# A graph-convolution and mixture-of-experts kernel: a 512-column clear on GpSimd after each gather of result rows

## The chip, the cores and the metric

The kernel runs on one core of one Trainium2 chip. The time is the device time of one launch in microseconds (us), and the number of a kernel is the median of its runs. Five engines run their own instruction streams and meet through semaphores: TensorE (PE in the profile), VectorE (DVE), ScalarE (ACT), GpSimd (POOL) and SyncE (SP), which here only starts transfers.

## The reference

```python
# x: 8192 x 128, adj: 8192 x 8192, all float32
x = x + gnn(layernorm(x), adj)            # message passing
x = x + moe(layernorm(x))                 # 16 experts, best 2 of them for each row

# gnn:  msg = z @ W + B
#       weights = where(adj < 1, exp(-(1/adj - 1)**2 / 0.5), 0);  return weights @ msg
# moe:  logits = z @ gate_w + gate_b;  top 2 experts, softmax over the two logits
#       h = relu(z @ w1[e] + b1[e]);  out = h @ w2[e] + b2[e]     (128 -> 256 -> 128)
#       y = z + sum of the two experts' outputs by their shares
#       return layernorm(y) * gamma + beta
```

## The kernel before, in words

The 8192 rows are 16 groups of 512 rows. **The main stage** runs over the groups and, for each, over 16 chunks of 512 columns of the adjacency matrix. SP loads a chunk, VectorE and ScalarE turn its values into weights (lines 654, 660, 516, 521), TensorE transposes them (L1137), ScalarE finishes them (L527), and TensorE multiplies them with the messages (L1118). When a group is done, its rows are normalised, the gate picks two experts for each row, and GpSimd scatters the group's rows to a DRAM array `rows_in`, sorted by expert, with eight indirect transfers of 128 rows each (L476).

**The expert stage** begins when the last group is nearly through, at about 1430 us. The sorted rows are cut into 153 units, each of one expert. The groups form three batches of 7, 5 and 4 groups, with 71, 35 and 47 units; units of the second batch have 256 rows, the others 128. For each unit SP loads the rows (L374), TensorE transposes them (L1153), ScalarE copies them out (L592), TensorE makes the first layer (L1164), ScalarE applies the ReLU (L601), TensorE makes the second layer (L1192), and VectorE adds the bias (`add_bias`, L989). SP stores the results of two units at a time to the DRAM array `rows_out` (L387). VectorE also copies each unit's weights out of the table of experts (`fetch`, L980).

**Gather and combine.** A group's results lie scattered in `rows_out`. Once all the units of a batch are stored, GpSimd fetches each of its groups with eight indirect transfers (K = 2 experts for each row, times TB = 4 tiles of 128 rows). Each transfer moves 128 rows of 512 bytes (L494), into one of four buffers `back`. From the fifth group on, GpSimd waits before a group until VectorE has used the buffer (`back_free`). One tiny multiplication, `carry()` (L457), precedes the eight. VectorE then combines the group in about a dozen steps (`combine_slot`, L1004 to L1028; its layer norm uses L666, L673 and L698 to L702, with two steps on ScalarE, L533/L535 and L613), and SP stores it.

**The order** is written out by hand. Each engine runs a loop over i = 0 to 231. In step i VectorE does `add_bias(i - 1)`, `fetch(i + 7)` and the step `i - starts[g]` of every group g whose combine is under way. `starts` is a list of constants: 79, 85, 91, 97, 103, 109, 120 for the first batch, 131, 142, 153, 164, 175 for the second, 186, 197, 208, 219 for the third. Seven groups are therefore combined from step 153 on, after the last unit. VectorE executes in this order, so a combine that waits for its gather (`back_in`) holds back the units behind it. In the profile `back`, `rin` and the other buffers of this stage appear under the name `chunk`, since they are cut from the chunks' storage.

Of the kernel before, what the change touches and what calls it, by code (L numbers as in the profile page):

```python
# [13 lines left out]
P = 128  # L14
# [5 lines left out]
def gnn_moe_kernel(nc, x, adj, gnn_w, gnn_b, gate_w, gate_b, w1, b1, w2, b2, gamma, beta, out):  # L20
    N, D = x.shape
    E, _, F = w1.shape
    FT = F // P
    K = 2
# [35 lines left out]
    KB = K * TB  # L60
# [12 lines left out]
    with ctx:  # L73
        def sb(name, shape, dt=F32):
            return ctx.enter_context(nc.sbuf_tensor(name, shape, dt))

        def sem(name):
            return ctx.enter_context(nc.semaphore(name))
# [15 lines left out]
        eps = sb("eps", [P, 1])  # L94
        zeros = sb("zeros", [P, UW // P * D])
        pool_carrier = sb("pool_carrier", [1, 3])
        iota_e = sb("iota_e", [P, E])
        upto_e = sb("upto_e", [P, E, E])
        region0 = sb("region0", [P, len(BATCHES), E])
# [119 lines left out]
        rows_ready = sem("rows_ready")  # L219
        carried = sem("carried")  # L220
        scattered = sem("scattered")
        spare_zero = sem("spare_zero")
        ends_ready = sem("ends_ready")
        padded = sem("padded")
# [66 lines left out]
        def _(sp):  # L291
# [36 lines left out]
            def pad(b, e):  # L328
                if e == 0:
                    sp.wait_ge(ends_ready, b + 1)  # L330
                    sp.wait_ge(zeros_ok, 2)
                    _, values = nc.values_load_multi_w_load_instructions(
                        ends[0:1, b, :], engines=[mybir.EngineType.SP], min_val=0, max_val=BASE[-1] - UW,
                        skip_runtime_bounds_check_because="a region's start plus the rows counted in it")
                    region_ends.update(zip(range(E), values))
                sp.dma_start(rows_in[bass.ds(region_ends[e], UR[b]), :].rearrange("(p t) d -> p (t d)", t=TILES[b]),
                             zeros[:, 0:UR[b]]).then_inc(padded, 16)
# [20 lines left out]
            def load_rows(u):  # L358
                b = batch_of(u)
                if u == UNIT0[b]:  # L360

                    sp.wait_ge(table_ready, b + 1)
                    sp.wait_ge(padded, (b + 1) * E * 16)
                    sp.wait_ge(scattered, FIRST[b + 1] * KB * 16)
                    sp.wait_ge(spare_zero, len(BATCHES) * 16)
                if u == UNIT0[b] or u % AT_ONCE == 0:
                    upper = min(u // AT_ONCE * AT_ONCE + AT_ONCE, UNIT0[b + 1])
                    _, values = nc.values_load_multi_w_load_instructions(
                        r_tab[0:1, u:upper], engines=[mybir.EngineType.SP], min_val=0, max_val=BASE[-1] - UW,
                        skip_runtime_bounds_check_because="the table is clamped to the batch's last rows")  # L370
                    unit_rows.update(zip(range(u, upper), values))
                if u >= RIN:
                    sp.wait_ge(rin_turned, u - RIN + 1)
                sp.dma_start(rin[u % RIN][:, 0:UR[b]],  # L374
                             rows_in[bass.ds(unit_rows[u], UR[b]), :].rearrange("(p t) d -> p (t d)", t=TILES[b])
                             ).then_inc(rin_full[u % RIN], 16)
# [48 lines left out]
        @block.gpsimd  # L425
        def _(pool):
            pool.memset(ident[:, :], 0.0).then_inc(blank, 1)
            pool.memset(before[:, :], 1.0).then_inc(blank, 1)
            pool.memset(ones[:, :], 1.0).then_inc(const_ok, 1)
            pool.memset(eps[:, :], EPS).then_inc(const_ok, 1)  # L430
            pool.memset(minus_half[:, :], -0.5).then_inc(const_ok, 1)
            pool.wait_ge(blank, 2)
            pool.affine_select(out=ident[:, :], in_=ident[:, :], compare_op=ALU.not_equal, fill=1.0,
                               base=0, pattern=[[-1, P]], channel_multiplier=1).then_inc(const_ok, 1)

            pool.affine_select(out=before[:, :], in_=before[:, :], compare_op=ALU.is_gt, fill=0.0,
                               base=0, pattern=[[1, P]], channel_multiplier=-1).then_inc(const_ok, 1)
            pool.memset(zeros[:, :], 0.0).then_inc(zeros_ok, 1)
            pool.memset(pool_carrier[:, :], 0.0).then_inc(zeros_ok, 1)
            pool.iota(iota_e[:, :], pattern=[[1, E]], base=0, channel_multiplier=0,  # L440
                      allow_small_or_imprecise_dtypes=True).then_inc(const_ok, 1)
            for b in range(len(BATCHES)):
                pool.iota(region0[:, b, :], pattern=[[REGION[b], E]], base=BASE[b], channel_multiplier=0,
                          allow_small_or_imprecise_dtypes=True).then_inc(const_ok, 1)
            pool.iota(unit_steps[:, :], pattern=[[P, max(BATCHES) * TB]], base=0, channel_multiplier=0,
                      allow_small_or_imprecise_dtypes=True).then_inc(const_ok, 1)
            pool.iota(unit_no[:, :], pattern=[[1, MOST]], base=0, channel_multiplier=0,
                      allow_small_or_imprecise_dtypes=True).then_inc(const_ok, 1)
            pool.wait_ge(zeros_ok, 2)

            for b in range(len(BATCHES)):
                pool.dma_start(rows_in[BASE[b + 1] - UR[b]:BASE[b + 1], :].rearrange("(p t) d -> p (t d)", t=TILES[b]),
                               zeros[:, 0:UR[b]]).then_inc(spare_zero, 16)

            def carry():

                pool.tensor_tensor(pool_carrier[0:1, 0:1], pool_carrier[0:1, 1:2], pool_carrier[0:1, 2:3],  # L457
                                   ALU.mult).then_inc(carried, 1)

            def guess(g):  # L460

                pool.wait_ge(const_ok, CONSTS)
                pool.wait_ge(mv_ready, GROUPS + g + 1)
                pool.tensor_scalar(spread[:, :], mv_now[:, 0, :, 1], EPS, None, ALU.add).then_inc(spread_ready, 1)  # L464
                pool.wait_ge(spread_ready, g + 1)
                pool.tensor_tensor(rs[:, 0, :], spread[:, :], minus_half[:, :], ALU.pow).then_inc(guessed, 1)

            for g in range(GROUPS):
                guess(g)
                if g:  # L470
                    pool.wait_ge(carried, g)
                pool.wait_ge(rows_ready, g + 1)
                carry()
                for k in range(K):
                    for b in range(TB):
                        pool.indirect_dma_start(  # L476
                            rows_in, bass.IndirectOffsetOnAxis(row_now[:, k, b:b + 1].bitcast(U32), 0),
                            y[:, b, :], None).then_inc(scattered, 16)

            def results_there(b):  # L480
                for i in range(RO):
                    pool.wait_ge(ro_out[i], (PAIR0[b + 1] - i + RO - 1) // RO * 16)

            for b, n in enumerate(BATCHES):
                for g in range(FIRST[b], FIRST[b + 1]):
                    pool.wait_ge(carried, GROUPS + g)
                    if g == FIRST[b]:
                        results_there(b)
                        pool.wait_ge(idx_ready, b + 1)
                    if g >= BACK:  # L490
                        pool.wait_ge(back_free, g - BACK + 1)
                    carry()
                    for kb in range(KB):
                        pool.indirect_dma_start(  # L494
                            back[g % BACK][:, kb, :], None, rows_out[b],
                            bass.IndirectOffsetOnAxis(row_back[:, g, kb:kb + 1].bitcast(U32), 0)).then_inc(back_in[g % BACK], 16)

        @block.scalar
        def _(act):
# [741 lines left out]
```

## Time and profile before

| | us |
|---|---|
| median of 3 runs | 1829.3 (1829.25 to 1834.15) |
| span of the profiled execution, first to last instruction | 1823.2 |
| PE busy | 1624.7 (89%) |
| ACT busy | 1565.7 (86%) |
| DVE busy | 1499.7 (82%) |
| POOL busy | 463.6 (25%) |
| 128 gathers of result rows (L494), busy | 122.3, mean 955 ns |
| 128 scatters of rows (L476), busy | 216.7, mean 1693 ns |

The page gives the profiled execution by its span; the runs' median is 6.1 us above that span. The shares are averages over two unlike stages: PE is busy nearly all the time until about 1430 us, and far less in the last 300 to 400 us, where units, gathers and combines run side by side. In the rows below "idle before" stands in square brackets behind an instruction, with what the profile takes to have ended it; "issue" means that nothing in the profile explains the wait, and "remote" that it was put down to an unknown queue.

### The profile page before, as it was taken

What the parts mean: (1) busy time and instruction counts of PE and PEld (TensorE: products, weight loads), DVE (VectorE), ACT (ScalarE), POOL (GpSimd) and SP (SyncE); (2) the same over time, 40 slices, a digit from 0 to 9 for tenths busy, and PEclk for the clock granted to TensorE, in tenths of its full rate; (3) what the DMA queues carried; (4) which work ended last, traced back from release to release, by engine and by line L of the source; (5) the groups of instructions that cost most, each with busy time, mean ns of one, the idle gap of its engine ahead of it and who ended that gap; (6) DMA issues with size and microseconds to landing.
All of it is one profiled execution on the core that took longest, in us unless ns stands there. A gap on an engine that the chain in (4) does not pass through costs nothing.

```text
span 1823.2 us, 24195 instructions
## 1 busy us (share of the span) xinstructions
PE 1624.7 (89%) x8178; PEld 1073.6 (59%) x8178; DVE 1499.7 (82%) x2298; ACT 1565.7 (86%) x1502; POOL 463.6 (25%) x342
## 2 busy tenths in 40 slices
PE   4999999999999999999999999999999987384720
PEld 3666666666666666666666656666666786373620
DVE  7999998989899999999999989999998443153464
ACT  5899999999999999999999999999999664253531
POOL 0001223131314040407132231313140213535342
PEclk9999999999999999999999999999999999696765
DMA  9559867676767676776776676787673244343431
GB/s 313 158 160 290 235 199 215 195 217 193 214 195 212 196 212 198 220 213 202 210 202 209 199 210 199 209 247 208 202 206 121 80 124 143 87 141 97 129 110 50
DMA packets 216792, 338.22 MB, mean 186 GB/s; under 512 B 18080, under 2 KB 74144, under 8 KB 216544
## 3 DMA queue, kind: packets, MB, share of 16 engines
q1 hardware_dynamic: 208368, 319.62, 59.8%
q0 software_dynamic: 8304, 17.06, 3.1%
q8 instruction: 68, 1.11, 0.2%
q14 instruction: 52, 0.43, 0.1%
HBM read 303.07 MB, written 33.55 MB: 185 GB/s over the span
## 4 chain that ended last, share of the span: by engine, by line
PE 84%; DVE 6%; another core or an unknown queue 5%; issue 3%; ACT 1%; DMA 1%; DVEq 0%; SPq 0%; ACTq 0%
PE acc L1118 48%; PE tp L1137 24%; PE tp L1164 4%; PE tp L1192 3%; PE acc L1192 2%; DVE chunk L654 1%; PE tp L1153 1%; DVE stats L666 1%; DVE chunk L660 1%; DVE chunk L1004 1%; PE misc L1094 1%; ACT chunk L613 1%; DVE msg L729 1%; DMA xs<-in_x_dram 1%
## 5 line engine op out<-in xcount | busy, mean ns | idle before, releaser
L1118 PE MATMUL acc<-wT,msg 128*128 128x512 f32 x2048 | 976.0, 599 | 0.0
L527 ACT ACTIVATE wT<-tp 128x1024 f32<-128x1024 f32 x512 | 761.0, 1674 | 14.0 <-PE tp L1137 12.4
L521 ACT ACTIVATE chunk<-chunk 128x2048 f32<-128x2048 f32 x256 | 655.3, 2560 | 0.1
L660 DVE SCALAR_TENSOR_TENSOR chunk<-chunk 128x2048 f32<-128x2048 f32 x256 | 584.8, 2284 | 54.7 <-ACT chunk L521 54.1
L1137 PEld LDWEIGHTS tp<-ident,chunk 128*128 128x128 f32 x4096 | 478.7, 141 | 223.2 <-issue 221.5
L654 DVE SCALAR_TENSOR_TENSOR chunk<-chunk 128x2048 f32<-128x2048 f32 x256 | 583.5, 2280 | 1.9 <-DMA chunk<-in_adj_dram 1.9
L1137 PE MATMUL tp<-ident,chunk 128*128 128x128 f32 x4096 | 534.3, 274 | 0.0
L516 ACT ACTIVATE chunk<-chunk 128x4096 f32<-128x4096 f32 x118 | 511.0, 4331 | 0.0
L1118 PEld LDWEIGHTS acc<-wT,msg 128*128 128x128 f32 x2048 | 349.1, 190 | 258.3 <-issue 245.8
L457 POOL TENSOR_TENSOR pool_carrier<-pool_carrier 1x1 f32<-1x1 f32 x32 | 43.7, 1365 | 951.5 <-DVE row_now L845 825.9
L476 POOL DMA_INDIRECT rows_in<-y,row_now x128 | 216.7, 1693 | 40.4 <-issue 40.4
L601 ACT ACTIVATE msg<-tp,chunk 128x128 f32<-128x128 f32 (+1 forms) x306 | 103.6, 392 | 80.2 <-PE tp L1164 41.0
L494 POOL DMA_INDIRECT chunk<-rows_out,row_back x128 | 122.3, 955 | 38.8 <-issue 37.6
L1164 PE MATMUL tp<-msg,chunk 128*128 128x128 f32 (+1 forms) x612 | 116.0, 315 | 0.0
L592 ACT ACTIVATE msg<-tp 128x128 f32<-128x128 f32 (+1 forms) x153 | 46.2, 303 | 79.0 <-remote 40.7
L464 POOL TENSOR_SCALAR spread<-mv_now 128x4 f32<-128x4 f32 x16 | 31.1, 1946 | 293.7 <-DVE mv_now L673 293.6
L1192 PE MATMUL tp<-blobs,msg 128*128 x376 | 61.9, 299 | 45.7 <-issue 29.3
L1192 PE MATMUL acc<-blobs,msg 128*128 x376 | 61.1, 297 | 43.3 <-DVE chunk L989 26.6
L1164 PEld LDWEIGHTS tp<-msg,chunk 128*128 128x128 f32 x612 | 92.9, 205 | 2.8 <-issue 0.5
L989 DVE TENSOR_TENSOR chunk<-acc,blobs 128x128 f32<-128x128 f32 (+1 forms) x76 | 24.2, 319 | 83.0 <-remote 56.7
L1192 PEld LDWEIGHTS tp<-blobs,msg 128*128 128x128 f32 x376 | 53.9, 208 | 51.3 <-issue 50.1
L989 DVE TENSOR_TENSOR chunk<-tp,blobs 128x128 f32<-128x128 f32 (+1 forms) x77 | 24.3, 316 | 71.8 <-remote 34.7
(121 smaller groups left out, 794.7 us busy)
## 6 DMA issues: line engine op xcount, KB each, us to landing
chunk<-in_adj_dram SPq DMA_DIRECT2D x256, 1024.0 KB, 5.4
chunk<-rows_in SPq DMA_DIRECT2D x118, 64.0 KB
rows_out<-chunk SPq DMA_DIRECT2D x59, 128.0 KB
chunk<-rows_in SPq DMA_DIRECT2D x35, 128.0 KB
rows_out<-chunk SPq DMA_DIRECT2D x17, 256.0 KB
y_kept<-y SPq DMA_DIRECT2D x16, 256.0 KB, 6.1
chunk<-y_kept SPq DMA_DIRECT2D x16, 256.0 KB
out_dram<-chunk SPq DMA_DIRECT2D x16, 256.0 KB
```

Source lines behind the costliest of these rows:

```text
L476: pool.indirect_dma_start(rows_in, bass.IndirectOffsetOnAxis(row_now[:, k, b:b + 1].bitcast(U32), 0), y[:, b, :], None).then_inc(scattered ...
L494: pool.indirect_dma_start(back[g % BACK][:, kb, :], None, rows_out[b], bass.IndirectOffsetOnAxis(row_back[:, g, kb:kb + 1].bitcast(U32), 0 ...
L516: act.activation(two, two, ACT.Ln, bias=TINY).then_inc(logged, 2)
L521: act.activation(slot(c), slot(c), ACT.Exp, scale=-1.0).then_inc(inverted, 1)
L527: act.activation(wT[:, (g * PPG + m) % WSLOTS, :], tp[(g * PPG + m) % TSLOTS][:, :], ACT.Exp, scale=-2.0).then_inc(weighted, 1)
L601: ins = act.activation(hT[u % HT][:, t * n:(t + 1) * n], h_bank[u % H_BANKS][:, t * n:(t + 1) * n], ACT.Relu, bias=slots[u % SLOTS][:, B1 ...
L654: dve.scalar_tensor_tensor(out=slot(c), in0=slot(c), scalar=1.0, in1=slot(c), op0=ALU.is_lt, op1=ALU.mult).then_inc(masked, 1)
L660: dve.scalar_tensor_tensor(out=slot(c), in0=slot(c), scalar=2.0, in1=slot(c), op0=ALU.subtract, op1=ALU.mult).then_inc(squared, 1)
L1118: ins = pe.matmul(acc[:, :], msg[:, n, :], wT[:, (g * PPG + m) % WSLOTS, k * ROWS:(k + 1) * ROWS], start=(n == 0), stop=(n == 2 * PPG - 1))
L1137: ins = pe.transpose(tp[s % TSLOTS][:, t * ROWS + b * P:t * ROWS + (b + 1) * P], chunk[:, c % RING, b, j:j + P], ident[:, :])
L1164: ins = pe.matmul(h_bank[u % H_BANKS][:, t * n:(t + 1) * n], slots[u % SLOTS][:, W1 + t * P:W1 + (t + 1) * P], rT[u % RT][:, 0:n], start=T ...
L1192: ins = pe.matmul(o_bank[u % O_BANKS][:, r:r + D], hT[u % HT][:, t * n + r:t * n + r + P], blobs[:, bass.ds(second_layers[u], 1), W2 + t * ...
```

## The change

Behind each of the 128 gathers GpSimd now clears a new scratch tile `pool_rest` of 128 partitions by 512 float32 columns, which nobody reads. Each clear counts a new semaphore `rested`, and each clear but the first waits until the one before it has counted. The tile takes 2048 bytes of each partition. No other engine's instructions change.

```diff
@@ -94,6 +94,7 @@
         pool_carrier = sb("pool_carrier", [1, 3])
+        pool_rest = sb("pool_rest", [P, 512])
@@ -219,6 +220,7 @@
         scattered = sem("scattered")
+        rested = sem("rested")
@@ -494,6 +496,9 @@
                         pool.indirect_dma_start(
                             back[g % BACK][:, kb, :], None, rows_out[b],
                             bass.IndirectOffsetOnAxis(row_back[:, g, kb:kb + 1].bitcast(U32), 0)).then_inc(back_in[g % BACK], 16)
+                        if g + kb:
+                            pool.wait_ge(rested, g * KB + kb)
+                        pool.memset(pool_rest[:, :], 0.0).then_inc(rested, 1)
```

## Rows read from the trace of the kernel before

**Rows 1.** The page: the span, from the first to the last instruction.
```profile
span 1823.2 us, 24195 instructions
```
**Rows 2.** Windows, L989 alone: stretch, length, busy (times), clock, DMA share, GB/s.
```profile
1529.40:1569.40 40.00, 1.27 (x3) 0.67 0.40 111
1581.90:1591.70 9.80, 0.85 (x2) 1.00 0.54 161
1601.90:1611.70 9.80, 1.23 (x3) 1.00 0.39 113
1618.70:1628.70 10.00, 1.27 (x3) 1.00 0.46 126
1650.00:1680.00 30.00, 1.45 (x5) 0.65 0.33 87
1696.50:1706.30 9.80, 1.12 (x4) 0.84 0.57 156
1717.60:1727.40 9.80, 1.11 (x4) 0.98 0.56 162
1529.40:1748.00 218.60, 26.83 (x79) 0.79 0.41 116
```
**Rows 3.** Timeline of POOL, two gathers, `carry()`, a gather: start, length, line.
```profile
1536.96 0.95 POOL L494 DMA_INDIRECT chunk<-rows_out,row_back  x1 [0.30 <-issue]
1538.22 0.94 POOL L494 DMA_INDIRECT chunk<-rows_out,row_back  x1 [0.30 <-issue]
1539.17 0.18 POOL L457 TENSOR_TENSOR pool_carrier<-pool_carrier 1x1 f32<-1x1 f32 x1
1539.50 0.98 POOL L494 DMA_INDIRECT chunk<-rows_out,row_back  x1
```
**Rows 4.** Timeline of ACT and DVE, after the longest run of gathers.
```profile
1574.51 0.38 ACT L592 ACTIVATE msg<-tp 128x256 f32<-128x256 f32 x1 [13.21 <-remote]
1574.57 0.42 DVE L989 TENSOR_TENSOR chunk<-acc,blobs 128x256 f32<-128x256 f32 x1 [27.41 <-remote]
```
**Rows 5.** Timeline of DVE, the same dependent step during gathers and after them.
```profile
1790.19 0.16 DVE L702 TENSOR_TENSOR rs<-rs,nt 128x4 f32<-128x4 f32 x1 [1.23 <-DVE nt L701]
...
1800.03 0.17 DVE L701 TENSOR_SCALAR nt<-nt 128x4 f32<-128x4 f32 x1
1800.23 0.16 DVE L702 TENSOR_TENSOR rs<-rs,nt 128x4 f32<-128x4 f32 x1
```
**Rows 6.** Windows, all engines, main stage: with eight scatters, and without.
```profile
217.30:233.40 16.10, 16.10 (x76) 9.86 (x75) 12.79 (x10) 16.10 (x13) 13.97 (x8) 1.00 0.77 225
189.00:205.10 16.10, 16.10 (x76) 9.78 (x76) 15.43 (x24) 16.10 (x12) 0.00 (x0) 1.00 0.87 248
```
**Rows 7.** Windows, L989 alone, expert stage: before, and during, the last eight scatters.
```profile
1476.00:1490.00 14.00, 4.07 (x14) 1.00 0.50 135
1490.00:1502.00 12.00, 1.17 (x4) 0.85 0.36 107
```
**Rows 8.** Timeline of POOL at the start: clears of 128 and of 256 columns.
```profile
0.94 0.20 POOL L428 MEMSET before<- 128x128 f32 x1
...
1.90 0.30 POOL L438 MEMSET zeros<- 128x256 f32 x1
2.15 0.09 POOL L439 MEMSET pool_carrier<- 1x3 f32 x1
```
**Rows 9.** Timeline of POOL, the last four groups: before and at their end.
```profile
1748.87 0.23 POOL L457 TENSOR_TENSOR pool_carrier<-pool_carrier 1x1 f32<-1x1 f32 x1 [21.49 <-DMA rows_out<-chunk]
...
1788.96 0.95 POOL L494 DMA_INDIRECT chunk<-rows_out,row_back  x1 [0.30 <-issue]
```
**Rows 10.** Timeline of DVE: combines of groups 11, 13 and 15 begin.
```profile
1763.71 2.32 DVE L1004 SCALAR_TENSOR_TENSOR chunk<-chunk,share 128x128 f32<-128x128 f32 x8
...
1795.30 2.31 DVE L1004 SCALAR_TENSOR_TENSOR chunk<-chunk,share 128x128 f32<-128x128 f32 x8
...
1811.98 2.31 DVE L1004 SCALAR_TENSOR_TENSOR chunk<-chunk,share 128x128 f32<-128x128 f32 x8
```

## The prediction

> **What bounds the kernel now.** I read the page first, for the span [rows 1], and then asked which part of it the change can reach. GpSimd makes no gather before 1529 us, so the first 1529 us stay as they are. What is left is 294 us: 218.6 us until the last unit, and 75.2 us in which only gathers and combines are left.
>
> Next come the windows of `add_bias` (L989), which runs once for each unit and so counts progress [rows 2]. Up to 1748 us GpSimd gathers in seven bursts, which are the first seven rows. Together they last 119.2 us, and 3+2+3+3+5+4+4 = 24 units are finished in them, or 0.20 units per us. The other 55 of the 79 units of the last row [rows 2] take the remaining 99.4 us, or 0.55 per us. So the expert stage runs at little more than a third of its pace while GpSimd gathers, although the transfers keep the DMA engines busy only 0.33 to 0.57 of the time, and TensorE's clock mostly stands at its upper level of 2.4 GHz in the short bursts.
>
> The timeline shows it from close by. After the burst of 32 gathers that ended at 1569.4, ScalarE and VectorE started again within 0.06 us of each other, at 1574.51 and 1574.57, after waits of 13.2 and 27.4 us [rows 4]. In the last burst even VectorE's dependence on itself becomes slow: L702 waits 1.23 us for L701, where after the gathers it starts 0.20 us behind it and waits for nothing that is shown [rows 5]. So what the bursts slow is the handing over between engines (semaphores or issue), and not one buffer or one transfer. I can't name the mechanism from the trace. I call it the jam.
>
> The Trainium skill ("SBUF — State Buffer", section "Who interferes with whom") says that PE and ACT never wait on anyone, and that only the port pair of VectorE and GpSimd contends. The trace disagrees as far as bursts of gathers go, since ScalarE sat still for 13.2 us beside them [rows 4].
>
> **How dense must GpSimd's work be to jam the others?** Two places help. In the main stage eight scatters took 16.1 us, one each 2.0 us, and PE and ACT were busy for all 16.1 us, just as in an equally long stretch without scatters [rows 6]. In the expert stage the last eight scatters fell within 12 us, and there L989 went from 14 in 14 us down to 4 in 12 us [rows 7]; the gathers come one each 1.25 us [rows 3]. So at that density the expert stage jams, and at 2.0 us the main stage, which has fewer handovers, doesn't. The change lands between the two.
>
> **The change, part by part.**
>
> *One clear.* A clear of 128 columns lasts 0.20 us and one of 256 columns 0.30; the instruction behind the latter starts 0.25 us after it [rows 8]. From 0.20 and 0.30, another 256 columns add 0.20, so 512 columns last about 0.50 us, and GpSimd is free for the next instruction after some 0.45. That is an estimate.
>
> *The spacing of gathers.* Now a gather starts 1.25 us after the one before: 0.95 of work and 0.30 without [rows 3]. `carry()` slips into this gap almost for nothing: it starts when the gather ends, and the next gather starts 0.33 us later, 1.28 us after its predecessor [rows 3]. Bounds for the clear: if all of it slipped into the gap but for what is longer than it, 0.45 - 0.30 = 0.15 us are added, spacing 1.40; if nothing did, 1.25 + 0.45 = 1.70. The gather after `carry()` starts 0.15 us after the carry's end, so I take 0.95 + 0.50 + 0.15 = 1.60 us. A burst then lasts 1.60/1.25 = 1.28 times as long.
>
> *The wait.* It is for the clear before, which ended a whole gather earlier (about 1 us). I cost it at nothing. Behind it stand only the clear and the next gathers. Were the counting itself jammed, the wait would space the gathers further, with no effect on the rest but theirs.
>
> *VectorE.* The clear shares a port with VectorE's copies. By the rule of the page named above, a copy in float32 and a GpSimd instruction exclude each other, and whichever comes second waits. No row shows this for a clear. From the durations of rows, a clear would be in the way 0.45 of 1.60 us; a copy (one for each of at most 71 units) that meets it loses at most 0.45, on average 0.22, so 71 x 0.28 x 0.22 = 4 us if all copies fell in bursts. Half of them do at most: 2 us. The bounds are 0 and 71 x 0.45 = 32 us.
>
> *Up to the last unit.* The seven bursts grow from 119.2 to 152.6 us. With r units per us in them and 0.553 outside, this part takes 152.6 + (79 - 152.6 r) / 0.553. For r = 0.20, as now, it is 239.9 us, 21 more than 218.6. It breaks even at r = 0.28. Without a jam r would be 0.50, the pace of 2 us for a unit of 256 rows, and the part would take 157.5 us, 61 less. Between these ends I assume that the others get on in proportion to the share in which GpSimd makes no descriptors: now 0.30 of 1.25 (24%), then 0.65 of 1.60 (41%). That gives r = 0.20 x 41/24 = 0.34 and 201.6 us: **17 us less**. This scaling is my choice, and the weakest step.
>
> *After the last unit.* The last 32 gathers begin 0.64 us after the `carry()` at 1748.87 and end at 1789.9 [rows 9]. At 1.60 us they end at 1749.5 + 51.2 = 1800.7; 1.7 us more for the last to land (the jam of [rows 5] was over that long after the last gather). Undisturbed, VectorE needs 8.34 us for a group (1795.30 to 1811.98 is two), but 31.6 us lie between the combines of groups 11 and 13 [rows 10], which is 14.9 too many. This jam set in late: group 11's combine began at 1763.71, which is just two undisturbed groups after the last unit (1748), so for the first 14 us of the burst at the least nothing was slowed, with VectorE, ScalarE and a few transfers as the only traffic. So 1.25 us is only just too dense for so little traffic, and at 1.60 I expect no jam. The last group is then combined from 1802.4, when it has landed, instead of 1811.98 [rows 10]: **9.6 us less**. What is late next is the gathers themselves.
>
> **Sum:** -17 - 9.6 + 2 = -24.6, so the profiled span goes from 1823.2 to 1798.6. The median lies 6.1 us above the span, which I keep: **1805 us**.
>
> **Rivals.**
>
> *The jam goes away altogether (1758).* For it: 1.25 us seems only just too dense, as the late start of the last jam shows [rows 9, 10], and 2.0 us does no harm in the main stage [rows 6]. Against: units hand over more often than the main stage does, and bursts of only 9.8 us jam too [rows 2]. Time: -61 up to the last unit, -9.6 behind it, or 1829.3 - 70.6 = 1758.7. Less isn't possible, since the 128 gathers in a row take 128 x 1.60 = 205 us from 1529.4 on, 1.7 to land, 11.2 for the last combine and the 6.1: 1753.
>
> *The jam lasts as long as the burst, and bursts are longer (1861).* The one mechanism on the slow side: GpSimd's gathers jam the others from their first few us to their last, whatever the spacing, so r stays 0.20: +21. In the last stretch group 13 can only be combined when all have landed, at 1802.4 instead of 1795.3 with a little to catch up, and the end moves by 11. 1829.3 + 32 = 1861. It decides if r stays below 0.28. For it: every burst so far ended jammed, and VectorE's copies are held besides. Against: the main stage [rows 6].
>
> *The clear doesn't space them (1829).* GpSimd hides most of the clear in the gap that exists, as it does `carry()` [rows 3], spacing 1.30 to 1.40; a slightly longer burst and a slightly lighter jam cancel. Against: 0.45 us don't fit into 0.30.
>
> **How the numbers follow.** 0.35 for the forecast, with its own range of 1785 to 1823; 0.25 for no jam; 0.30 for the jam as long as the burst, with all that leads above 1835; 0.10 for hardly any effect. One can tell 0.3%, 5.5 us, from no change. Faster: 0.35 + 0.25 = 0.60. Same: 0.09 of the last. Slower: 0.30 and the rest of the last, 0.31. The range goes down to 1757, which takes in most of the no-jam case, and up to 1852, which leaves out the upper half of the slow case.
>
> **What would show it.** Spacing of gathers in the timeline: 1.6 us, with a clear of about 0.5 between. L989 in the bursts, 0.34 per us; 0.20 would prove the slow rival, 0.5 the fast one. Dependent steps of VectorE around the last burst without waits of 1.2 us, and the last combine starting right after the last gather lands. I am wrong if the spacing is right and the pace in the bursts doesn't rise, or if the time changes before 1529 us.

## The result, and the profile after

The changed kernel takes **1766.45 us** (median of 4 runs, 1766.04 to 1767.87) against 1830.3 before (median of 4 as well), a ratio of 0.9649 with a 95% interval of 0.9636 to 0.9663. I had forecast 1805: the sign was right and the size wrong, a loss of 64 us where I had 25. The rival without any jam, at 1758, came much nearer.

The head of the page of the changed kernel, with its two costliest POOL lines of the last stage. L496 is the gather (L494 before) and L501 the clear; other lines have moved by 5 (L989 is L994, L1004 is L1009).

```profile
span 1764.5 us, 24323 instructions
PE 1612.9 (91%) x8178; PEld 1064.6 (60%) x8178; DVE 1513.4 (86%) x2298; ACT 1567.8 (89%) x1502; POOL 539.1 (31%) x470
...
L496 POOL DMA_INDIRECT chunk<-rows_out,row_back x128 | 128.1, 1000 | 20.7 <-issue 20.7
...
L501 POOL MEMSET pool_rest<- 128x512 f32 x128 | 70.6, 552 | 0.1
```

GpSimd does 75 us more work, and the span is 58.7 us shorter than the 1823.2 of [rows 1]. The timeline of POOL shows the new rhythm, which answers to [rows 3]:

```profile
1537.69 0.95 POOL L496 DMA_INDIRECT chunk<-rows_out,row_back  x1 [0.16 <-issue]
1538.63 0.54 POOL L501 MEMSET pool_rest<- 128x512 f32 x1
1539.34 0.95 POOL L496 DMA_INDIRECT chunk<-rows_out,row_back  x1 [0.16 <-issue]
...
1750.66 0.95 POOL L496 DMA_INDIRECT chunk<-rows_out,row_back  x1 [0.16 <-issue]
```

One gather each 1.65 us, where I had 1.60. The clear starts the moment the gather ends (the page has 0.1 us of idle time before all 128 together), so its wait is never seen. The windows of `add_bias`, which answer to [rows 2]: stretch, length, busy (times), clock, DMA share, GB/s.

```profile
1530.00:1570.00 40.00, 7.46 (x18) 1.00 0.68 196
1530.00:1669.80 139.80, 26.67 (x80) 0.96 0.62 174
1669.80:1764.50 94.70, 0.00 (x0) 0.50 0.27 75
```

(In the last stretch TensorE has nearly nothing left to do, and its granted clock falls to 0.50, the level of 1.2 GHz.) In the first 40 us of gathers 18 units are finished, where it was 3. All the rest of the units are done in 139.8 us with GpSimd gathering throughout: 0.57 per us, where the bursts before had 0.20 and the pauses between them 0.55. The last unit ends at 1669.8 instead of 1748. But the stretch behind it, where I expected a gain, grew from 75.2 to 94.7 us. The timeline of DVE, where the combines of the last groups begin, says why. It answers to [rows 10].

```profile
1684.46 2.33 DVE L1009 SCALAR_TENSOR_TENSOR chunk<-chunk,share 128x128 f32<-128x128 f32 x8 [5.08 <-DMA chunk<-rows_out,row_back]
1698.14 2.31 DVE L1009 SCALAR_TENSOR_TENSOR chunk<-chunk,share 128x128 f32<-128x128 f32 x8 [5.07 <-DMA chunk<-rows_out,row_back]
...
1753.25 2.32 DVE L1009 SCALAR_TENSOR_TENSOR chunk<-chunk,share 128x128 f32<-128x128 f32 x8 [5.04 <-DMA chunk<-rows_out,row_back]
```

In this stretch each group waits 5 us for its gather, and the groups come 13.7 us apart instead of 8.34. GpSimd gathers without a pause from 1531 to 1751.6, and the end follows 13 us later. So the bound has moved: the kernel now ends as soon as 128 gathers and their clears allow. The chain of waits agrees. POOL had no share of it before; the shares by engine are now:

```profile
PE 80%; POOL 11%; DVE 4%; issue 2%; DMA 1%; another core or an unknown queue 0%; ACT 0%; SPq 0%; POOLq 0%; ACTq 0%; DVEq 0%
```

### The profile page after: what moved, and what is told of

Its sections match the earlier page's. It is cut to its first block, busy times and chain, and to the rows that moved or that the text cites. A ratio compares the mean times of both kernels' runs of the same rounds, so it can differ in the third digit from the quotient of the medians.

```text
span 1764.5 us, 24323 instructions
## 1 busy us (share of the span) xinstructions
PE 1612.9 (91%) x8178; PEld 1064.6 (60%) x8178; DVE 1513.4 (86%) x2298; ACT 1567.8 (89%) x1502; POOL 539.1 (31%) x470
## 3 DMA queue, kind: packets, MB, share of 16 engines
q0 software_dynamic: 8304, 17.06, 3.2%
## 4 chain that ended last, share of the span: by engine, by line
PE 80%; POOL 11%; DVE 4%; issue 2%; DMA 1%; another core or an unknown queue 0%; ACT 0%; SPq 0%; POOLq 0%; ACTq 0%; DVEq 0%
PE acc L1123 49%; PE tp L1142 24%; POOL chunk L496 7%; POOL pool_rest L501 4%; PE tp L1169 2%; DVE chunk L659 1%; PE tp L1197 1%; PE acc L1197 1%; DVE chunk L665 1%; PE misc L1099 1%; DVE stats L671 1%; DVE msg L734 1%; DMA xs<-in_x_dram 1%; PE misc L1073 1%; PE tp L1158 1%
## 5 line engine op out<-in xcount | busy, mean ns | idle before, releaser
L496 POOL DMA_INDIRECT chunk<-rows_out,row_back x128 | 128.1, 1000 | 20.7 <-issue 20.7
L1169 PE MATMUL tp<-msg,chunk 128*128 128x128 f32 (+1 forms) x612 | 111.7, 307 | 0.0
L1169 PEld LDWEIGHTS tp<-msg,chunk 128*128 128x128 f32 x612 | 89.1, 198 | 2.4 <-issue 0.5
L1009 DVE SCALAR_TENSOR_TENSOR chunk<-chunk,share 128x128 f32<-128x128 f32 x128 | 36.3, 345 | 54.4 <-DMA chunk<-rows_out,row_back 54.2
L501 POOL MEMSET pool_rest<- 128x512 f32 x128 | 70.6, 552 | 0.1
L538 ACT ACTIVATE lnv<-mv_now,eps 128x4 f32<-128x4 f32 x16 | 4.7, 296 | 69.7 <-DVE mv_now L678 63.2
```

The costliest lines, as they stand in the source:

```text
L496: pool.indirect_dma_start(back[g % BACK][:, kb, :], None, rows_out[b], bass.IndirectOffsetOnAxis(row_back[:, g, kb:kb + 1].bitcast(U32), 0 ...
L501: pool.memset(pool_rest[:, :], 0.0).then_inc(rested, 1)
L1169: ins = pe.matmul(h_bank[u % H_BANKS][:, t * n:(t + 1) * n], slots[u % SLOTS][:, W1 + t * P:W1 + (t + 1) * P], rT[u % RT][:, 0:n], start=T ...
```

## The experiments

They are taken by question. The kernels ran on several chips, and the kernel before took 1829 to 1830 us on some and 1824.5 to 1825 on others, so every ratio is against the kernel before on the same chip. Two kernels timed on different chips are compared by their ratios: what is called "by the ratios" below is the difference of two ratios times the 1827 us or so of the kernel before, and it is uncertain by some 4 us, as the intervals say.

**Is it the spacing of the gathers, and where is the edge?** Five kernels differ from the changed one in the length of the clear alone. The edit, here for one column:

```diff
-        pool_rest = sb("pool_rest", [P, 512])
+        pool_rest = sb("pool_rest", [P, 1])
```

One column. 

> The clear behind each gather is cut to 1 column; the count and the wait stay, so gathers should come one each 1.28 to 1.35 us instead of 1.25 (before) and 1.68 (changed). Density theory (the jam comes from GpSimd making descriptors for too large a share of the time): jams as before, 1815 to 1835 us, L994 at 0.20 to 0.25 per us in the bursts. Rival, any instruction or a wait between two gathers is enough: no jam, and 1700 to 1740 us, as 128 gathers at 1.3 us need only 166 us.

256 columns. 

> Clear of 256 columns, about 0.30 us, gathers one each 1.42 us. If the jam falls steadily with density (my prediction's scaling by the free share): still jammed, and slower than with 512 columns, 1770 to 1800 us. If there is a threshold and it lies below 1.42 us: no jam, and since the changed kernel is bound by its gathers, 128 x (1.68 - 1.42) = 33 us less than 1766, about 1733 us.

320 columns. 

> Clear of 320 columns, gathers one each 1.52 us. Known so far: 1.46 us jams in part (1790 us), 1.58 us doesn't (1751 us). If the edge is sharp and lies below 1.52: 128 x 0.06 = 8 us less than with 384 columns, 1743 us. If the jam grows steadily from 1.58 downwards: 1755 to 1780 us.

384 columns. 

> Clear of 384 columns, about 0.43 us, gathers one each 1.56 us. With 256 columns (1.46 us) VectorE still showed waits of 2 to 6 us, with 512 (1.68 us) none. If the jam's edge lies below 1.56: bound by gathers, 128 x 0.12 = 15 us less than 1766, about 1751 us. If between 1.56 and 1.68: 1765 to 1785 us.

1024 columns. 

> Clear of 1024 columns, about 1.0 us, gathers one each 2.1 us. Both theories: no jam, the gathers in a row bind, so 128 x (2.1 - 1.68) = 54 us more than the changed kernel, about 1820 us. Less than 10 us more would mean that the gathers don't bind it.

The spacing is that of two gathers of a group in the timeline, and the units are the L994 from 1530 to 1570 us. The waits are VectorE's before L994 from 1529 us on, as far as the profile puts them down to an unknown queue ("remote"), added up. They come and go with the jam.

| clear | spacing, us | units in 40 us | "remote" waits, us | time, us | before, same chip | ratio (95% interval) |
|---|---|---|---|---|---|---|
| none (before) | 1.25 | 3 | 83.8 | 1829.05 | | |
| 1 column | 1.25 | 3 | 99.2 | 1831.09 | 1829.05 | 1.001 (0.9998 to 1.0022) |
| 256 | 1.45 | 8 | 61.0 | 1789.77 | 1829.05 | 0.9778 (0.975 to 0.9806) |
| 320 | 1.50 | 18 | 6.7 | 1746.52 | 1824.66 | 0.9572 (0.9556 to 0.9588) |
| 384 | 1.58 | 17 | 0 | 1751.25 | 1824.45 | 0.9602 (0.9586 to 0.9618) |
| 512 | 1.65 | 18 | 0 | 1766.45 | 1830.3 | 0.9649 (0.9636 to 0.9663) |
| 1024 | 2.1 | 14 | 0 | 1823.31 | 1829.05 | 0.9966 (0.9957 to 0.9976) |

(For 384 and 1024 columns the 40 us begin at 1529.4; a unit more or less at the edges of a window means nothing.) One column slips into the gap of 0.30 us whole and does nothing, although it brings the instruction and the wait: that rival falls. Between 1.45 and 1.50 us the pace jumps from 8 to 18 units, and the waits fall from 61.0 to 6.7 us. (The 1790 us at 256 columns alone would have fitted the steady rise too; the kernel with 320 decides it.) So there is an edge, and not the slope that I had assumed. It isn't quite a clean one: at 320 columns the later units, of 128 rows, still have some of these waits. From 1610 to 1650 us 23 of them are finished, against 31 with 384 columns, and the last unit ends at 1683.9 instead of 1663.3. That costs something: before the last batch GpSimd waits 6.86 us for results, where with 384 columns it doesn't wait. The median came out 5 us below that of 384 columns, where I had 8. (The profiled execution took 1751.2 us and was the slowest of its four.)

```profile
DVE chunk L994 <- remote: 61.0, 18, 6.4
```
```profile
DVE chunk L994 <- remote: 6.7, 6, 2.2
```
```profile
1685.62 0.23 POOL L459 TENSOR_TENSOR pool_carrier<-pool_carrier 1x1 f32<-1x1 f32 x1 [6.86 <-DMA rows_out<-chunk]
```

(Waits of the whole stage: us in total, times, the longest; at 256 columns, and then at 320. The third line is the timeline of POOL at 320.) Above the edge the time follows the gathers. From the first gather to the last it takes 219.7 us with 512 columns and 206.9 with 384, 12.8 less where I had 15. In time, 384 columns gain 9 us by the ratios; that their median fell on the 1751 that I had expected is in part the chip's doing. 1024 columns bring back nearly all that was won. At 256 columns it is still the jam. These are lines of DVE at 256 columns, and then at 320:

```profile
1538.91 0.43 DVE L994 TENSOR_TENSOR chunk<-tp,blobs 128x256 f32<-128x256 f32 x1 [3.84 <-remote]
1543.44 0.42 DVE L994 TENSOR_TENSOR chunk<-acc,blobs 128x256 f32<-128x256 f32 x1 [3.89 <-remote]
1554.56 0.42 DVE L994 TENSOR_TENSOR chunk<-acc,blobs 128x256 f32<-128x256 f32 x1 [6.37 <-remote]
```
```profile
1553.19 0.42 DVE L994 TENSOR_TENSOR chunk<-acc,blobs 128x256 f32<-128x256 f32 x1 [0.48 <-remote]
...
1554.87 0.42 DVE L994 TENSOR_TENSOR chunk<-tp,blobs 128x256 f32<-128x256 f32 x1
1555.21 0.71 DVE L985 COPY chunk<-blobs 128x258 f32 x1
```

**Mean density, or from one gather to the next?** The same 128 clears, but eight in a row after the eight gathers of a group:

```diff
-                        if g + kb:
-                            pool.wait_ge(rested, g * KB + kb)
-                        pool.memset(pool_rest[:, :], 0.0).then_inc(rested, 1)
+                        for r in range(KB if kb == KB - 1 else 0):
+                            if g + r:
+                                pool.wait_ge(rested, g * KB + r)
+                            pool.memset(pool_rest[:, :], 0.0).then_inc(rested, 1)
```

> The same 128 clears, but eight in a row after a group's eight gathers, which then come one each 1.25 us for 10 us. If the mean density over 14 us counts: as the changed kernel, 1760 to 1775 us. If the density from one gather to the next counts, as the bursts of only 9.8 us in the kernel before suggest: each group jams after some 3 us and frees in the 4 us of clears, 1795 to 1830 us.

1793.1 us, ratio 0.9829 (0.9812 to 0.9846), 2 us below the range that I gave for it: the expected jam within each group, of which the clears then undo a part. DVE in this kernel, where the eight gathers of the first group run from 1530.34 to 1540.12:

```profile
1534.74 0.42 DVE L995 TENSOR_TENSOR chunk<-acc,blobs 128x256 f32<-128x256 f32 x1 [2.99 <-remote]
1541.92 0.42 DVE L995 TENSOR_TENSOR chunk<-tp,blobs 128x256 f32<-128x256 f32 x1 [6.55 <-remote]
```

So eight gathers in a row are already too many at 1.25 us; the clears have to stand between them.

**Is it the clear's writes, or the wait?** First one partition instead of 128:

```diff
-                        pool.memset(pool_rest[:, :], 0.0).then_inc(rested, 1)
+                        pool.memset(pool_rest[0:1, :], 0.0).then_inc(rested, 1)
```

> The clear of 512 columns writes one partition instead of 128; it should last the same 0.55 us. If only the time between gathers counts: as the changed kernel, 1760 to 1772 us. Rival, what helps is that the clear's 128-partition writes hold something off (VectorE's port, SBUF): jams again in part, 1790 to 1830 us.

1761.17 us, ratio 0.9654 (0.9637 to 0.9671). The clear lasts 529 ns instead of 552 and does the same. Then the same with eight places in a tile of 1024 columns, and only a group's first clear waiting:

```diff
-                        if g + kb:
-                            pool.wait_ge(rested, g * KB + kb)
-                        pool.memset(pool_rest[:, :], 0.0).then_inc(rested, 1)
+                        if kb == 0 and g:
+                            pool.wait_ge(rested, g * KB)
+                        pool.memset(pool_rest[kb // 2 * 32:kb // 2 * 32 + 1, kb % 2 * 512:kb % 2 * 512 + 512], 0.0).then_inc(rested, 1)
```

> As the run whose clears write one partition, but a group's eight clears go to eight places, and only the first of them waits for the ones before; 112 of the 127 waits are gone. If the wait is only there for order and the time between gathers does all: 1761 us as that run, within 3 us. Rival, the wait itself spaces or releases something: 1775 us or more.

1765.93 us, ratio 0.9677 (0.9661 to 0.9694): 5 us more than the kernel with all waits, a little beyond the 3 us that I allowed, but the jam is gone without them too: neither kernel has any of the table's waits. I don't claim that the wait gives 5 us: the two were timed on different chips, and their intervals overlap.

**What in a gather makes the jam?** Three kernels without clears, as before, whose gathers move less. The edit for 64 rows, with 16 in place of `P // 2` for sixteen; the combine's two additions (L1004) are cut to the same partitions:

```diff
-                            back[g % BACK][:, kb, :], None, rows_out[b],
-                            bass.IndirectOffsetOnAxis(row_back[:, g, kb:kb + 1].bitcast(U32), 0)).then_inc(back_in[g % BACK], 16)
+                            back[g % BACK][0:P // 2, kb, :], None, rows_out[b],
+                            bass.IndirectOffsetOnAxis(row_back[0:P // 2, g, kb:kb + 1].bitcast(U32), 0)).then_inc(back_in[g % BACK], 16)
```

and for half the bytes (half of each row is left out, and the two additions read the other half twice):

```diff
-                            back[g % BACK][:, kb, :], None, rows_out[b],
+                            back[g % BACK][:, kb, 0:D // 2], None, rows_out[b].rearrange("r (h d) -> (r h) d", h=2),
```

> The kernel before, without clears; each gathered row has 64 instead of 128 columns, so 256 bytes, with as many rows (half of the gathered data is left out, and the combine reads the other half twice). Gathers should still come one each 1.25 us. If the jam is made by the bytes moved: gone, 1720 to 1760 us. If by the number of rows or by GpSimd's work: as before, 1815 to 1835 us.

> The kernel before, without clears; each gather fetches 64 rows of 512 bytes instead of 128 (the other half is left out, and the combine's two additions work on 64 partitions). If the jam goes by the number of row descriptors for each us, and GpSimd needs the same 0.95 us for a gather: gone or much less, 1700 to 1760 us. If it goes by the share of time in which GpSimd makes descriptors, whatever their number: as before, 1815 to 1835 us.

> The kernel before, without clears; each gather fetches 16 rows of 512 bytes instead of 128 (the rest is left out, and the combine's two additions work on 16 partitions). With 64 rows the gathers still came one each 1.20 us and the stage jammed as before. If the jam comes with each gather instruction, whatever it moves: jammed again, 1815 to 1840 us. If it comes with the rows or descriptors, and 64 rows were only still too many: gone or much less, under 1780 us.

| gather | its length, us | spacing, us | units in 40 us | "remote" waits, us | time, us | ratio (95% interval) |
|---|---|---|---|---|---|---|
| 128 rows of 256 bytes | 0.94 | 1.25 | 3 | 92.7 | 1824.47 | 0.9997 (0.9987 to 1.0007) |
| 64 rows of 512 bytes | 0.90 | 1.20 | 2 | 98.6 | 1833.47 | 1.0045 (1.0031 to 1.0058) |
| 16 rows of 512 bytes | 0.84 | 1.15 | 3 | 103.7 | 1838.62 | 1.0074 (1.0056 to 1.0093) |

Neither bytes nor rows matter. With an eighth of the rows the jam is as bad, and the kernels with shorter gathers are even slower, in line with their denser spacing. So what counts belongs to the gather instruction and not to its load. These kernels don't tell apart three readings of that: how many gathers start in a given time, the share of the time in which GpSimd is within one (76% before, 73% with sixteen rows, 66% at 256 columns and 63% at 320), and the pause from the end of one to the start of the next (0.30 us, 0.50 at 256 columns, 0.55 at 320). The window of `add_bias` with sixteen rows:

```profile
1530.00:1570.00 40.00, 0.91 (x3) 0.63 0.18 51
```

The DMA share is down to 0.18, and still only three units pass.

**The terms one by one.** Clears behind the last batch's 32 gathers alone, then behind the first two batches' 96 alone (the other value of `b` in the condition, and the count of the wait set to match):

```diff
-                        if g + kb:
-                            pool.wait_ge(rested, g * KB + kb)
-                        pool.memset(pool_rest[:, :], 0.0).then_inc(rested, 1)
+                        n_rest = (g - FIRST[2]) * KB + kb
+                        if b == 2:
+                            if n_rest:
+                                pool.wait_ge(rested, n_rest)
+                            pool.memset(pool_rest[:, :], 0.0).then_inc(rested, 1)
```

> Clears of 512 columns behind the 32 gathers of the last batch alone. My prediction's term for the stretch after the last unit: 9.6 us less than before, 1820 us, the first 96 gathers jamming as before. Rival, the last stretch gains nothing because its gathers take longer: 1829 us or more.

> Clears of 512 columns behind the gathers of the first two batches only; the last 32 come one each 1.25 us. The last batch's gathers then end 32 x 0.43 = 14 us sooner: 1766 - 14 = 1752 us if they don't jam. If they jam as in the kernel before (15 us late): 1765 to 1770 us.

Last batch alone: 1822.19 us, ratio 0.9961 (0.995 to 0.9972), so 7 us less where I had 9.6. First two alone: 1758.51 us, ratio 0.9635 (0.9619 to 0.9651), the whole gain of the change and perhaps a little more (3 us by the ratios, within their noise). Its last gathers jam as before, but late. VectorE has these lines after group 14's additions begin at 1730.06, and the last gather starts at 1738.05:

```profile
1735.39 0.87 DVE L673 BATCH_NORM_STATS2 stats<-chunk 128x6 f32<-128x128 f32 x4 [1.76 <-remote]
1738.08 0.38 DVE L680 BATCH_NORM_AGGREGATE mv_now<-stats 128x2 f32<-128x6 f32 x4 [1.82 <-remote]
1742.15 0.16 DVE L705 SCALAR_TENSOR_TENSOR nt<-mv_now,rs 128x4 f32<-128x4 f32 x1 [3.69 <-ACT rs L542]
```

I had expected either 1752 without a jam or 1765 with the whole of it, and both came from the 1766 of a chip that is 5 us slower. So the median alone can't decide, but the trace can: the last gather starts 12.6 us sooner than in the changed kernel, and from its end to the end of the span it is 18.4 us instead of 12.9. A short jam takes back 5.5 us of what the denser gathers gain.

**Can one have more?** The scatters of the last two groups jam the units too [rows 7]. A clear behind each of them (the waits of the gathers' clears count these 16 too, here and in the two kernels after it):

```diff
                             y[:, b, :], None).then_inc(scattered, 16)
+                        if g >= 14:
+                            n_rest = (g - 14) * KB + k * TB + b
+                            if n_rest:
+                                pool.wait_ge(rested, n_rest)
+                            pool.memset(pool_rest[:, :], 0.0).then_inc(rested, 1)
```

> The changed kernel, with the same clear also behind the 16 scatters of the last two groups, which fall into the expert stage. The same jam should go there: 4 units in 12 us became the pace, and at about 1 per us some 5 us are to be had before the first gather, so everything from there on 3 to 7 us earlier, 1760 to 1763 us. Rival, the scatters end later and the second batch's rows with them: no change or slower.

1756.48 us, ratio 0.9628 (0.9612 to 0.9644): 4 us less than the changed kernel by the ratios, as expected, though the two intervals overlap. (The medians are 10 us apart, but not of one chip.) The jam in the scatters is gone for certain. The windows of `add_bias` over the 12 us of [rows 7], and the first `carry()` of the gathers, in this kernel:

```profile
1490.00:1502.00 12.00, 3.40 (x12) 1.00 0.49 140
```
```profile
1520.18 0.18 POOL L459 TENSOR_TENSOR pool_carrier<-pool_carrier 1x1 f32<-1x1 f32 x1 [16.64 <-DMA rows_out<-chunk]
```

Twelve units instead of four, and the first `carry()` starts at 1520.2 instead of 1530.3. Then shorter clears in the tail, and last all three together:

```diff
-                        pool.memset(pool_rest[:, :], 0.0).then_inc(rested, 1)
+                        pool.memset(pool_rest[:, 0:(256 if g >= 10 else 384)], 0.0).then_inc(rested, 1)
```

(In the first of the two, 512 stands for 384.)

> As the run with clears behind the last scatters, but from group 10 on, when the last unit is nearly done, the clears have 256 columns. 48 gathers come 0.22 us sooner each: 10 us less than that run, about 1751 us, if light traffic doesn't jam at 1.46 us. Rival, VectorE's combines jam: no gain.

> Clears of 384 columns, of 256 from group 10 on, and of 512 behind the last 16 scatters. The gains measured one by one were 15 us (384 for 512), 10 us (scatters) and 10 us (256 from group 10 on; 5 of it are left from 384): 1766 - 15 - 10 - 5 = 1736 us if they add. Rival, they take from the same waits: 1745 us.

1746.74 us, ratio 0.9575 (0.9559 to 0.9591), and **1739.29 us**, ratio 0.9532 (0.9516 to 0.9548). The first is 10 us faster than the kernel with clears behind the scatters, on the same chip, so the tail bears the density at which units jam. The last is 3 us above the 1736 that I had added up. By the ratios it gains 21 us on the changed kernel, where the three gains add up to some 18 (9, 4, and the half of 10 that I count as left from 384 columns), so they add within the noise. This is the fastest version run.

## Why the prediction was right and wrong

- *GpSimd's bursts jam the other engines, and thinning them out helps.* Right. It is shown by the lengths of the clear and by the clears in one block.
- *One clear, its spacing, its wait.* The clear is 10% longer than I had it, 0.55 us for 0.50, and the spacing right within 3%, 1.65 for 1.60; the wait costs nothing that shows. Over all 128 gathers the mean is (1750.66 - 1530.96) / 127 = 1.73 us, since `carry()` and gathers of up to 1.45 us come on top.
- *Up to the last unit, 17 us less.* **This is the step that failed.** I let the others' pace rise with the share of time that GpSimd leaves free, r = 0.34 units per us. It was 0.57. The jam has an edge, between 1.45 and 1.50 us; 1.65 is past it, and so this stretch lost 78 us. Below the edge the rule does well: at 256 columns GpSimd leaves 0.50 of 1.45 us free, which gives 0.29 per us, and 42 units in the 138 us of gathers are 0.30. At 320 columns it gives 0.31 (0.55 of 1.50 us), and 75 units in 148 us are 0.51. I also capped the free pace at 0.50, that of 256-row units; the later units of 128 rows are faster, 27 from 1610 to 1650 us in the changed kernel. The late onset of the last jam, which I had read as "only just too dense", pointed to an edge close by; I gave it to a rival instead of the forecast.
- *After the last unit, 9.6 us less.* As a change of its own it was nearly right (7 us, the interval says 5 to 9). In the sum it was wrong: with the units done 78 us sooner, the stretch is filled by gathers that are still to come, and grew by 19.5 us. I had named the gathers as what is late next, and worked out for the no-jam rival that 128 of them need until 1753. With the measured 1.73 instead of 1.60 us that bound is 1753 + 128 x 0.13 = 1770, where 1766 was measured. That bound, and not my sum, was the forecast to make.
- *VectorE's copies, 2 us.* The Trainium skill ("SBUF — State Buffer", "Who interferes with whom") has copies and GpSimd's instructions exclude each other. The trace agrees: the mean copy (L985) takes 363 ns instead of 293, and 619 with 1024 columns. That is 153 x 0.07 = 11 us of VectorE's time, more than my 2 and less than my bound of 32. What it costs the kernel no run separates; at its end VectorE waits for gathers anyway. The section's other sentence, that PE and ACT never wait on anyone, stands among rules for these ports. My prediction read ScalarE's 13.2 us [rows 4] as against it, but the profile puts that wait down to an unknown queue and not to a port, so the row neither bears the sentence out nor refutes it.
- *The rivals.* The slow one and the one without spacing fall with the result. (The 11 us that the slow one had behind the last unit don't come out of its own times, 1802.4 for 1795.3, which give 7.) The no-jam rival had it right that the jam goes, but that its time came within 8 us was luck in part: of its two terms, 61 us less were 78 less, and 9.6 less were 19.5 more. It was kept near by lying just above the bound of the gathers.

What in a gather instruction holds up the other engines is not settled. It isn't the bytes, the rows or the DMA engines' time. Whether it is GpSimd's own work or what each gather posts to the queues, whatever its size, no run here separates. The second stays possible: on its page the queue that carries the gathers (q0) has 8304 packets with 128 rows and with sixteen alike, while its bytes fall from 17.06 to 9.72 MB. Fewer rows did not mean fewer packets. The pauses were also always filled with clears; a pause of another kind was not tried.

## What to carry to other kernels

Where several engines stop and start together beside a dense run of GpSimd's indirect transfers, try spacing these: measure the pace of the others at two or three spacings, since the effect may have an edge, and take the shortest spacing beyond it. Put the spacing between the single transfers; behind a block of eight the same clears won half as much. When a jam goes away, work out the next bound before adding up gains, because gains of later stretches may then no longer count.

## What the hardware showed that I had not expected

- Gathers at 1.25 us each cut the expert stage from 18 units in 40 us to 3, and at 1.50 us each they cut nothing in these 40 us and little later (6.7 us of "remote" waits in all, against 83.8). The step from 8 to 18 units lies within 0.05 us.
- An indirect gather costs GpSimd 0.84 us for 16 rows, 0.90 for 64 and 0.94 for 128, so nearly all of it is fixed.
- A clear of 512 columns lasts nearly as long on one partition (529 ns) as on 128 (552 ns), and a clear of one column behind a gather doesn't space the gathers (1.25 us with and without).
